# Another fixed order of the same jobs: two attention layers, a quantized FFN and a dense mixture of experts on one core

## The reference, cut to what matters

```python
x = x + xattn0(layernorm(x), ctx)     # q from x; k, v from ctx; softmax over the 77 rows; output projection
x = x + ffn0(layernorm(x))            # both operands rounded to 8 bits with one scale for the whole tensor
x = x + xattn1(layernorm(x), ctx)     # as xattn0, no biases
x = x + experts(layernorm(x))         # 8 experts of 128 -> 256 -> 128, all of them on all tokens, gelu, summed
```

## Time and profile before

| | us |
|---|---|
| time, median of 3 executions | 409.39 (409.24 to 411.62) |
| span of the profiled execution | 411.6 |

### The profile page before, as it was taken

The page is one execution under the profiler, slowest core; times in us unless marked ns, Lnnn a source line. Parts: engine busy times, 40 slices in busy tenths (PEclk is TensorE's granted clock), DMA queues, the critical chain, the costliest instruction groups (busy, mean ns, idle before and its releaser), DMA issues.

```text
span 411.6 us, 4782 instructions
## 1 busy us (share of the span) xinstructions
PE 309.9 (75%) x1455; PEld 184.4 (45%) x1455; DVE 267.8 (65%) x682; ACT 167.3 (41%) x261; POOL 91.0 (22%) x87
## 2 busy tenths in 40 slices
PE   0068689978888843712657698989889999999995
PEld 0046333343434431202234334444437868888883
DVE  1576555367663736985677734766348799988883
ACT  0232152333546313863112334554664445454542
POOL 1511037001010205931110700101010653330600
PEclk9999985589999965855555559999999999999999
DMA  4338421030000091030230200200000000000000
GB/s 143 88 65 175 105 58 28 6 77 2 6 4 5 15 236 40 0 103 2 58 91 7 60 21 14 71 6 2 7 0 2 1 2 25 2 1 25 2 25 25
DMA packets 15902, 16.53 MB, mean 40 GB/s; under 512 B 3435, under 2 KB 11804, under 8 KB 15878
## 3 DMA queue, kind: packets, MB, share of 16 engines
q1 hardware_dynamic: 14834, 13.71, 14.0%
q0 software_dynamic: 704, 2.12, 2.0%
q10 hardware_dynamic: 340, 0.40, 0.3%
HBM read 4.53 MB, written 1.05 MB: 14 GB/s over the span
## 4 chain that ended last, share of the span: by engine, by line
PE 58%; DVE 25%; DMA 6%; ACT 6%; issue 3%; POOL 1%; SPq 0%; ACTq 0%; DVEq 0%; POOLq 0%
PE ps_acc L1092 11%; PE ps_tok L941 6%; PE ps_key L950 5%; DVE mx L645 5%; DMA wkv<-in_wkv 5%; PE ps_acc L1062 4%; PE ps_acc L1064 3%; PE ps_acc L1063 3%; DVE xn L571 3%; DVE stats L561 3%; PE ps_m L958 2%; PE ps_m L980 2%; PE ps_tok L1049 2%; PE ps_tok L1051 2%; DVE axb L849 2%
## 5 line engine op out<-in xcount | busy, mean ns | idle before, releaser
L645 DVE TENSOR_REDUCE mx<-ps_tok 128x4 f32<-128x312 f32 x128 | 57.4, 477 | 38.3 <-PE ps_tok L941 37.4
L441 ACT ACTIVATE big<-ps_key 104x512 f32<-104x512 f32 x96 | 55.3, 596 | 54.1 <-PE ps_key L950 52.8
L941 PE MATMUL ps_tok<-kst,qst 97*128 97x312 f32 x128 | 59.0, 487 | 14.7 <-DVE mx L645 14.2
L334 POOL TENSOR_SCALAR veps<-mv 128x4 f32<-128x4 f32 x16 | 3.7, 229 | 247.8 <-DVE mv L564 247.8
L941 PEld LDWEIGHTS ps_tok<-kst,qst 97*128 97x128 f32 x128 | 30.8, 247 | 52.6 <-DVE mx L645 27.0
L950 PE MATMUL ps_key<-qst,kst 105*104 105x512 f32 x96 | 45.3, 483 | 3.9 <-ACT big L441 1.9
L787 DVE TENSOR_TENSOR qst<-big,qst 128x512 fp32r<-128x512 f32 x64 | 44.3, 692 | 2.2
L785 DVE CAST qst<-big 128x512 fp32r<-128x512 f32 x64 | 27.0, 422 | 9.7 <-ACT big L505 9.5
L571 DVE TENSOR_SCALAR xn<-x,mv,rstd 128x128 f32<-128x128 f32 x64 | 27.5, 595 | 8.8 <-POOL rstd L335 8.8
L505 ACT ACTIVATE big<-ps_tok,b 128x512 f32<-128x512 f32 x32 | 22.0, 689 | 25.1 <-PE ps_tok L1051 24.9
L1092 PE MATMUL ps_acc<-big,vbd 104*32 104x512 f32 x192 | 30.5, 712 | 0.7 <-ACT big L441 0.7
(11 more groups left out here) (192 smaller groups left out, 543.5 us busy)
## 6 DMA issues: line engine op xcount, KB each, us to landing
qst<-qhi SPq DMA_DIRECT2D x64, 64.0 KB, 2.0
kst<-rbuf SPq DMA_DIRECT2D x24, 156.0 KB, 3.0
qst<-qlo SPq DMA_DIRECT2D x32, 64.0 KB, 2.0
w1f<-in_w POOLq DMA_DIRECT2D x2, 1024.0 KB, 7.9
x<-in_x SPq DMA_DIRECT2D x4, 256.0 KB, 10.5
out<-xn SPq DMA_DIRECT2D x4, 256.0 KB, 2.3
qst<-mthl SPq DMA_DIRECT2D x32, 16.0 KB
wqo<-in_wqo SPq DMA_DIRECT2D x1, 256.0 KB, 7.1
```

The costliest lines, as they stand in the source:

```text
L441: act.activation(p[:, j, :], key[n % 2][0:PR, :], ACT.Exp, scale=SCALE).then_inc(q["p_ready"], 1)
L645: nc.vector.tensor_reduce(mx[:, u % 2, t, g, 0, :], tok[n % 2][:, 0:KG].rearrange("p (j h) -> p h j", h=HG), AX.X, ALU.max).then_inc(q["to ...
L941: mm(tok[n % 2][:, 0:KG], qst[0:MASKROW + 1, s, g, 128 * t:128 * t + 128], kst[0:MASKROW + 1, b, g, :], start=True, stop=True).then_inc(q[ ...
```

## The change

It replaces the numbers of all the tables. No instruction is added or taken away, no wait is changed in code, and the lists of POOL and SP keep their order. One of the tables tells what the rest are like:

```diff
-        BESIDE = dict(krow=[-31.4, -27.9, -9.9, 6.1], vr0=[-28.6, -25, -12.2, -10.4], lnstat=[-34.5, -26, -12, 4], lnx0=[-34, -23, -8, 8],
-                      nt=[29.8, 46.3, 62.3, 78.3], round=[12, 20, 28], wqt=[46, 48, 51, 53], kt=[55], vr=[56.1, 58, 60.8, 62.1])
...
+        BESIDE = dict(
+            krow=[-25.935, -25.174, -2.306, 12.108],
...
+            round=[15.43, 22.386, 28.123],
```

More of the change, by code:

```diff
@@ L200, in build @@
         UNITS = range(B)
-        AT = (dict(
-            xt=[-32.1],
-            q=[-29.6],
-            tok=[-15.5 + 0.75 * c for c in range(NT * G)],
-            max=[-4],
-            key=[2 + j for j in range(NC * G)],
-            pv=[7.1, 8.1, 11.4, 12.1, 15.1, 16.1],
-            copy=[17.2],
-            on=[20.1],
-            ot=[21.3],
-            wo=[24],
-            ln=[26.4],
-        ), dict(
-            xt=[-32.3],
-            q=[-29.3],
-            tok=[-15.5 + 0.75 * c for c in range(NT * G)],
-            max=[-3.9],
-            key=[2 + 0.85 * j for j in range(NC * G)],
-            pv=[6.2, 8.1, 11.1, 11.9, 15.1, 16.1],
-            copy=[17.2],
-            on=[19.7],
-            ot=[21.7],
-            wo=[23.8],
-            ln=[26.8],
-        ))
@@ L232, in build @@
-        BESIDE = dict(krow=[-31.4, -27.9, -9.9, 6.1], vr0=[-28.6, -25, -12.2, -10.4], lnstat=[-34.5, -26, -12, 4], lnx0=[-34, -23, -8, 8],
-                      nt=[29.8, 46.3, 62.3, 78.3], round=[12, 20, 28], wqt=[46, 48, 51, 53], kt=[55], vr=[56.1, 58, 60.8, 62.1])
-        FFN = dict(hround=[-42, -41, -15, -5], down=[-40.1, -31.7, -13.1, -3.1], lnx=[-37.6, -25, -9, 4],
-                   gset=[30], x1=[31.1, 48.6], experts=[64.5 + 0.914 * n for n in range(NH)])
+        AT = (
+            dict(
+                xt=[-31.526],
+                q=[-29.598],
+                tok=[-15.5 + 0.75 * c for c in range(NT * G)],
+                max=[-3.969],
+                key=[2.58 + 0.907 * j for j in range(NC * G)],
+                pv=[7.1, 8.1, 11.4, 12.1, 15.1, 16.1],
+                copy=[16.611],
+                on=[19.77],
+                ot=[21.6],
+                wo=[23.473],
+                ln=[26.517],
+            ),
+            dict(
+                xt=[-31.134],
+                q=[-26.882],
+                tok=[-15.5 + 0.733 * c for c in range(NT * G)],
+                max=[-1.966],
+                key=[2 + 0.85 * j for j in range(NC * G)],
+                pv=[6.081, 8.881, 10.981, 11.781, 14.981, 15.981],
+                copy=[17.823],
+                on=[19.7],
+                ot=[21.762],
+                wo=[23.236],
+                ln=[27.442],
+            ),
+        )
@@ new lines, in build @@
+        BESIDE = dict(
+            krow=[-25.935, -25.174, -2.306, 12.108],
+            vr0=[-29.38, -24.665, -12.096, -11.168],
+            lnstat=[-37.276, -28.314, -11.348, 3.598],
+            lnx0=[-34.125, -20.72, -8.352, 7.308],
+            nt=[30.586, 46.3, 61.193, 78.3],
+            round=[15.43, 22.386, 28.123],
+            wqt=[44.799, 46.799, 51.175, 51.799],
+            kt=[54.862],
+            vr=[57.506, 58.396, 62.166, 63.506],
+        )
+        FFN = dict(
+            hround=[-41.919, -41, -15.721, -6.97],
+            down=[-40.1, -36.159, -13.1, -2.765],
+            lnx=[-36.574, -24.612, -9.133, 3.867],
+            gset=[18.811],
+            x1=[32.55, 48.155],
+            experts=[68.391 + 0.992 * n for n in range(NH)],
+        )
@@ L242, in build @@
         AT_YT, AT_Y, AT_LOG, AT_A, AT_B, AT_C = HLAG + 2, HLAG + 3, 12, 13, 15, 5
         FIRST_LOG, FIRST_A, FIRST_B, FIRST_C = 5, 6, 8, 12
-        ACT_LATE = dict(copy=0.4, key=0.2)
-        DVE_LATE = dict(on=0.1)
+        ACT_LATE = dict(copy=0.116, key=0.245)
+        DVE_LATE = dict(on=0.207)
         def order(L, late={}):
```

## The result

| | before | after |
|---|---|---|
| median of the executions, us | 410.5 (409.24 to 413.8, 4 of them) | 397.92 (396.22 to 398.9, 4 of them) |
| span of the profiled execution, us | 411.6 | 395.8 |
| mean granted clock in it, as the page has it | 0.854 | 0.903 |

The ratio of after to before is 0.968, with a 95% interval of 0.961 to 0.974.

The account below looks back on a forecast made before the run. PE was taken as the bound, nearly so inside units, with waits for DVE and half-clock stretches to win. Terms -1.7, -0.8, -0.2, -1.5, -1.2, -0.5 sum to -5.9; 1.0 given back: 409.4 - 4.9 = 404.5 us, range 400.5 to 409.0.

Parts of the forecast that it names:

- the clock in unit 4: Layer 1, unit 4: clock rises at about 243 instead of 246.6 us, -1.5, bounds 0 and -4.
- the overlap ahead of it: Start of layer 1 to first `pv`: `lnx3` overlaps `w2l` 0.8 us instead of 3.1; net -0.2 with late `mthl`.
- the argument against the early clock: Unit 4: 10.6 us of saturated PE work had not lifted the clock until 246.6.
- `down3` ahead of `max0`: Start of layer 1: makes unit 4's `mthl` 4.5 us later, given back by less `lnx3` overlap and moved `q2`.
- `round1`: Layer 0: moved behind `on0` on DVE, so `ot0` comes earlier; -1.7 us.
- The clock behind it: Layer 0, after the wait before `ot0`: half-clock fall might vanish; bounds 0 and -1.5, taken as 0 for the median.
- The end of layer 0: `mthl2` to first `hround`: -0.4 forecast, the rest of the -0.8 for smaller layer 0 moves.
- The joints of layer 1: Waits for `mthl` and `qlo` at `xt3`, `x1` and `on0`, 1.99 us, removed; 60% counted, -1.2.
- Into the experts: Behind layer 1's last `pv`: PE idles 1.5 us instead of 2.0 with `on3` moved; -0.5.
- The 1.0 given back: Whole kernel: 1.0 us added back to the sum for small waits overlooked at new neighbours.
- clock up early and for good: Rival: `q2` lifts the clock before unit 4's first `pv`, no fall at 90; 401.2 us, chance 0.15.
- gains are not on the path: Rival: other waits replace the removed ones, about -2.2 us, so 407.2; chance 0.28.

Follow-up runs that it names:

- i3: The changed kernel run again unaltered, six executions on one chip: median 399.82 us, ratio 0.970 to the kernel before.
- c1: Kernel before, with POOL holding `w2h` and `w2l` until `lnx3` is done: 409.4 us, ratio 0.995.
- u2: Changed kernel with `down3` of layer 1 put back behind `max0`: 406.0 us.
- h2: Kernel before with two edits, `w2h` and `w2l` held until `lnx3` is done and layer 1's `q2` behind unit 4's fourth `key`: 404.0 us, ratio 0.984.
- i1: Kernel before with only `q2` of layer 1 moved behind the fourth `key` of unit 4: 411.0 us, ratio 0.999.
- h3: Changed kernel with `down3` back behind the maxima and `w2h` and `w2l` held until `lnx3` is done: 396.5 us, ratio 0.967.
- f1: Kernel before with only the start of layer 1 reordered (`hround`, `down`, `lnx`, first `xt` and `q`, `max0`): 406.8 us, ratio 0.994.
- e1: Kernel before with only `round1` moved, behind `tok2.7` on DVE instead of ahead of `on0`: 410.8 us, ratio 1.001.
- e2: Kernel before with the changed tables and late shifts for layer 0 only: 405.4 us, ratio 0.983.
- u3: Changed kernel with the first expert steps as before, four of them ahead of `on3`: 400.0 us.
- g1: Kernel before with only `x1` part 0, `xt3` and `q3` of layer 1 moved: 410.5 us, ratio 0.999.

## Why the prediction was wrong

**The step that failed is the clock in unit 4, with the overlap ahead of it.** C and D together gave -6.1, where -1.7 was forecast. Cut at the first `pv`, this is two terms, each too small by some 2 us. I had the mechanism of the clock: no hole, `q2` right before the first `pv`, an earlier rise. I sized it at -1.5, with the rise at about 243, though the rise right at the first `pv` stood in the text as the bound of -4. From the first `pv` to `mthl5` the kernel before takes 13.3 us and the changed one 9.5, so the term is -3.8; the clock was up at 227.2, ahead of the first `pv`. In i3, where it rose 1.3 us behind the first `pv`, the term is -3.4. The other term, which I had at -0.2, is -2.3: `mthl4` is 3.1 later and not 4.5, and the first `pv` came 5.2 us behind the first `key` instead of 6.0 (10.6 before), all of it at half clock. What led me astray was the argument against the early clock: "10.6 saturated us did not lift it until 246.6". c1 shows why it did not hold: 16.5 us of that work do not lift it either. It was no evidence on what happens with `q2` late and no hole. The two edits, of which the text named both, had to be taken as one step with two outcomes, and not as a rise that slides from 246.6 to 243.

**`down3` ahead of `max0`: right in kind, too dear.** C grew by 3.1 us, not by 4.5. DVE's wait of 1.18 and its 2.66 for `down3` came close to what was booked, but the 0.5 by which `tok0.11` was to be late was a gain of 0.6 instead (u2, with `down3` back, has 39.1 against 39.7). The price did not stay, as I had it, because of `lnx3` and `w2l`. Row first: the same four instructions take 1.11 us apart from `w2l` (c1, h2), 2.14 with a short overlap (after), 3.96 before, and 5.78 and 5.89 when `w2l` starts soon behind the first of them (u2, i1). In u2 `lnx3` begins at 222.06 and ends at 227.84, 0.58 after `w2l`. The Trainium skill ("SBUF — State Buffer", section "SBUF: two separate sides") has the later one block completely, and these rows agree. u2 shows that `down3` is even needed in this order; h3, that it is not once `w2l` is held.

**`round1` and the other moves in stage A: right.** Forecast -1.7 for `round1`, measured 1.5 between f1 and e1. The wait before `ot0` is 0.61, under the 1 us named. At a rise near 84.3 us stage A takes 51.6 in the old order (f1) and 49.4 in the new one (i3): 2.2 for all moves, where 2.1 was forecast. But the 0.38 at the first `key` brought only 0.1 (`mthl0` to `mthl1` takes 23.8 in f1 and e1, 23.7 in i3 and e2): in its place PE waits 0.31 us for a maximum (51.62 in after). The rest came with moves that I had not counted.

**The clock behind it: taken at 0 for the median, and that was wrong.** Stage A gave -4.3, of which the moves are 2.2. The missing fall is 1.6 or more, the short rise at 55.6 in before takes 0.5 of it back, and the last 1.1 is a rise at 80.4 instead of 84.3 in the one execution of after, a phase that i3 did not have. The fall belongs to the old joint (6 of 7), so it should have been counted for the median too, at the bound of -1.5 rather than at 0.

**The end of layer 0: -2.4 instead of -0.4.** Half of it is order and half is the clock. I had the value projection (its wait fell by 0.6) but had not looked at unit 3. Timeline of the kernel before, with the joint of after above (124.73) to compare:

```profile
127.14 0.45 PE L950 MATMUL ps_key<-qst,kst 105*104 105x512 f32 x1 [0.81 <-ACT big L441]
...
129.95 0.66 PE L973 MATMUL ps_m<-cst,tbuf 128*128 128x128 f32 x4 [0.92 <-DVE tbuf L660]
...
148.49 1.12 PE L973 MATMUL ps_m<-cst,tbuf 128*128 128x128 f32 x4 [1.38 <-DVE tbuf L660]
...
150.29 2.08 PE L980 MATMUL ps_m<-wqo,tbuf 128*128 128x128 f32 x8 [0.69 <-ACT tbuf L467]
```

Here 1.73 us of waits became 0.36 and the 0.24 ahead of `on2`, 1.1 us less, by `xt`, `on` and `ot` at their new places, which my walk through the lists had treated as nothing. Not all of these waits were on the path: from `mthl2` to `on3` after is 1.2 us shorter, not 1.7. The other 1.2 us are the clock at `ot3` and `wo3`. Timeline of after:

```profile
143.10 0.66 PE L982 MATMUL ps_m<-cst,tbuf 128*128 128x128 f32 x4 [1.38 <-DVE tbuf L669]
...
144.44 1.37 PE L989 MATMUL ps_m<-wqo,tbuf 128*128 128x128 f32 x8 [0.69 <-ACT tbuf L476]
```

In before the clock fell at 147.8, ahead of both, and in after at 145.3, behind most of `wo3`. That is a phase again: from `ot3` to the end of `wo3` it is 2.7 us in after, 3.3 in i3, 3.2 in e2 and 3.9 in before. e2 and i3 show 1.7 to 1.9 us for the stage rather than 2.4.

**The joints of layer 1: half right.** -0.7 instead of -1.2. The waits went as forecast, but g1 shows that most of them come back at the transfer behind `mthl` and ahead of `q3`: 0.3 us was left of 1.34 in unit 5. The 60% were too much.

**Into the experts: -2.6 instead of -0.5.** The waits gave 0.5 (u3). 1.3 more is PE's busy time for the same instructions (110.4 us in before, 109.1 in after), which a walk through waits can't see; u3 has 1.0 of it. The last 0.8 is in other small waits; 0.46 of it is a wait of a `key` for ACT at 300.12 in the trace of before that is in neither u3 nor after.

**The 1.0 given back** for overlooked waits had the wrong sign: in this case the overlooked places (unit 3, the experts) were gains. The rival "clock up early and for good" named what happened, with 0.15 (in i3 the rise came 1.3 us behind the first `pv`, and not before it), and even its 401.2 was too slow by the terms for the order ahead of that `pv`, the end of layer 0 and the experts. The rivals "gains are not on the path" and "slower" are excluded, the first one but for the joints. The time that I gave the first was also added up wrongly: the halves named make 1.85, so 407.5 and not 407.2.

## What to carry to other kernels

A term that depends on the granted clock is not a small correction to a sum of waits: here it was the largest single miss, and it flips as a whole, so give it two values with chances, not one in between; that PE was busy and the clock did not rise is no argument against a rise once the order changes. Where a step is booked as a price because it delays something, ask also which collision it moves apart, and try to remove the collision itself; that was the better kernel here.
